# Second gate/up tile of the first feed-forward layer as seven block products

## The reference

```
x = x + L0_ffn(L0_cond(x))          # LoRA with 8 routed experts, then 4-bit weights
x = x + L1_ffn(L1_cond(x))          # one of 8 weight matrices per batch, then RMSNorm and FFN

def L0_ffn(x):                      # HIDDEN 512, INTER 1376
    w_gu = scale[g] * (nibble - (zero[g] + 1))
    gate, up = split(x @ w_gu)
    h = silu(gate) * up
    return h @ w_d                  # w_d: 4-bit too
```

## Time and profile before

| what | value |
|---|---|
| median of 3 runs | 446.32 us (446.04 to 447.08) |
| profiled execution | 446.06 us, span 444.3 us |
| TensorE busy | 439.1 us, 99% of the span |
| VectorE busy | 341.6 us, 77% |
| ScalarE busy | 219.4 us, 49% |
| GpSimd busy | 188.9 us, 43% |
| granted TensorE clock | 0.999 |

### The profile page before, as it was taken

How to read it: one execution, slowest core, us unless ns; L and a number is a source line. 1 busy time by engine, 2 the same in 40 slices (tenths; PEclk the granted TensorE clock), 3 DMA queues, 4 the chain that set the end, 5 groups by cost and what they waited for, 6 DMA issues and landing times.

```text
span 444.3 us, 5507 instructions
## 1 busy us (share of the span) xinstructions
PE 439.1 (99%) x1946; PEld 358.6 (81%) x1946; DVE 341.6 (77%) x439; ACT 219.4 (49%) x283; POOL 188.9 (43%) x167
## 2 busy tenths in 40 slices
PE   8999999999999999999999999999999999999997
PEld 4688888888888888888888778888888888888885
DVE  4689997788777978948778567868688678999922
ACT  5415755666542213347677656466466554474200
POOL 2077887855008201900005778886997300000000
PEclk9999999999999999999999999999999999999999
DMA  8765133100008694386279517947668146986623
GB/s 292 182 210 162 44 105 107 49 1 1 1 4 276 191 352 204 131 327 252 97 260 333 211 47 238 287 166 217 226 212 273 63 137 261 351 288 177 231 90 142
DMA packets 30344, 79.96 MB, mean 180 GB/s; under 512 B 2497, under 2 KB 15585, under 8 KB 28657
## 3 DMA queue, kind: packets, MB, share of 16 engines
q1 hardware_dynamic: 26464, 68.04, 45.0%
q0 software_dynamic: 3280, 10.83, 7.8%
q10 hardware_dynamic: 576, 0.80, 0.6%
HBM read 58.95 MB, written 20.72 MB: 179 GB/s over the span
## 4 chain that ended last, share of the span: by engine, by line
PE 98%; DMA 1%; ACT 0%; DVE 0%; issue 0%
PE ps L1890 10%; PE ps L1892 10%; PE ps L1891 10%; PE ps L1635 10%; PE ps L1639 10%; PE ps L1636 10%; PE ps L1994 5%; PE ps L1992 5%; PE ps L1752 5%; PE ps L1750 5%; PE ps L1751 5%; PE ps L1993 5%; PE ps L1873 2%; PE ps L1871 2%; PE ps L1872 2%; DMA res<-in_xT 1%
## 5 line engine op out<-in xcount | busy, mean ns | idle before, releaser
L1635 PE MATMUL ps<-h_hi,ring_hi 128*128 128x512 f32 x152 | 59.1, 389 | 0.0
L1636 PE MATMUL ps<-h_lo,ring_hi 128*128 128x512 f32 x152 | 59.1, 389 | 0.0
L1088 DVE TENSOR_TENSOR ring_lo<-raw,ring_hi 128x1792 fp32r<-128x1792 f32 (+1 forms) x23 | 47.6, 2073 | 14.7 <-ACT ring_hi L725 14.7
L1890 PE MATMUL ps<-zt_hi,ring_hi 128*128 128x512 f32 x140 | 54.5, 390 | 0.4 <-issue 0.4
L1892 PE MATMUL ps<-zt_hi,ring_lo 128*128 128x512 f32 x140 | 54.5, 389 | 0.0
L1891 PE MATMUL ps<-zt_lo,ring_hi 128*128 128x512 f32 x140 | 54.5, 389 | 0.0
L1639 PE MATMUL ps<-h_hi,ring_lo 128*128 128x512 f32 x152 | 47.8, 389 | 0.0
L725 ACT ACTIVATE ring_hi<-raw 128x1792 fp32r<-128x1792 f32 (+1 forms) x23 | 36.7, 1594 | 22.3 <-PE ps L1892 10.1
L1636 PEld LDWEIGHTS ps<-h_lo,ring_hi 128*128 128x128 f32 x152 | 28.5, 188 | 6.0
L1635 PEld LDWEIGHTS ps<-h_hi,ring_hi 128*128 128x128 f32 x152 | 28.5, 188 | 5.9
L1639 PEld LDWEIGHTS ps<-h_hi,ring_lo 128*128 128x128 f32 x152 | 28.5, 188 | 5.9
(11 more groups left out here) (252 smaller groups left out, 1115.3 us busy)
## 6 DMA issues: line engine op xcount, KB each, us to landing
ad_raw<-in_w1T SPq DMA_DIRECT2D x8, 1024.0 KB, 6.3
wd<-down_weights SPq DMA_DIRECT2D x7, 1024.0 KB, 5.5
down_weights<-dhi SPq DMA_DIRECT2D x7, 896.0 KB, 4.4
down_weights<-dlo SPq DMA_DIRECT2D x7, 896.0 KB, 4.3
raw<-in_gu SPq DMA_DIRECT2D x12, 512.0 KB, 3.7
wd<-down_weights SPq DMA_DIRECT2D x7, 768.0 KB, 5.1
draw<-in_d SPq DMA_DIRECT2D x7, 512.0 KB, 5.4
dn_work<-in_qw_dn SPq DMA_DIRECT2D x11, 256.0 KB, 4.7
```

Of the source, the lines that this page charges most:

```text
L1088: dve.tensor_tensor(dst, src, hi_part.bitcast(F32), ALU.subtract).then_inc(done_sem, 1)
L1635: pe.matmul(ps[:, bank + hf, :], w_hi, v_hi[:, t], start=first, stop=False)
L1636: pe.matmul(ps[:, bank + hf, :], w_hi, v_lo[:, t], start=False, stop=False)
L1890: pe.matmul(ps[:, bank, :], ring1_hi[s][:, w], z_hi[:, t], start=first and k == 0, stop=False, skip_group_check=True)
```

## The change

Tile 1 becomes a block tile (`BLOCK_TILES` from 1, `PLAIN` without it), with frame number 0 of the block tiles. What its frame needs is written in front of the loop: TensorE issues its six products without a product 4 of a predecessor, ScalarE and VectorE get its snapshots, additions, silus and product. On GpSimd `sums_gu(1)` is added and the gathers of pair 2 move behind it, those of pair 4 ahead of `sums_gu(3)`. On ScalarE `w_hi(1)` moves behind the splits of y, and `w_hi(2)` ahead of tile 1's snapshots. On VectorE `w_lo(1)` moves behind the splits of y, the dequantisation of tile 3 behind the low part of the third activation sum, and tile 0's low part of h into tile 2.

```diff
@@ -57,10 +57,10 @@
 YT = 11
 ZW = FT0 * 16
 
-BLOCK_TILES = tuple(range(2, FT0 - 2))
+BLOCK_TILES = tuple(range(1, FT0 - 2))
 NS = len(BLOCK_TILES)
 S_COL = {B_S1: 8 * P, B_S2: 10 * P, B_S3: 12 * P}
-PLAIN = (0, 1, FT0 - 2, FT0 - 1)
+PLAIN = (0, FT0 - 2, FT0 - 1)
 NPAIRS = FT0 // 2
 TD_GROUPS = (2, 2, 4, 3)
 
@@ -160,7 +160,7 @@
         scale = [region(kb, f"scale{j}", [P, KD, 4 * P], F32) for j, kb in enumerate((108, 48, 108, 48, 56))]
         scale.append(region(64, "scale_last", [P, KD, 2 * P], F32))
         nib = region(116, "nib", [P, FT0 * 2 * P], F32)
-        sil = {i: region(kb, f"sil{i}", [P, T], F32) for i, kb in zip(PLAIN, (100, 104, 180, 172))}
+        sil = {i: region(kb, f"sil{i}", [P, T], F32) for i, kb in zip(PLAIN, (100, 180, 172))}
         y_raw = region(184, "y_raw", [P, KD, T], F32)
         yt_hi = region(0, "yt_hi", [P, 4, 2, HALF], F32R)
         yt_lo, yt_raw = region(16, "yt_lo", [P, 4, 2, HALF], F32R), region(16, "yt_raw", [P, 4, 2, HALF], F32)
@@ -667,15 +667,16 @@
                 pool.wait_ge(s_wf, i + 1)
                 sums(sum_at("q", i), *blocks0(i % 2))
 
-            for j in range(3):
-                scales_gu(j)
+            scales_gu(0)
+            scales_gu(1)
+            sums_gu(1)
+            scales_gu(2)
             sums_gu(2)
+            scales_gu(4)
             sums_gu(3)
             scales_gu(3)
             pool.dma_start(lnb[:, :], a["lnw"].partition_broadcast(P)).then_inc(s_ln, 16)
             sums_gu(4)
-            scales_gu(4)
-            sums_gu(5)
             scales_gu(5)
             for i in BLOCK_TILES[4:]:
                 sums_gu(i)
@@ -824,24 +825,29 @@
                 act.activation(snap0[i % 2][:, 1, :], snap0[i % 2][:, 1, :], ACT.Silu).then_inc(s_silu1, 1)
 
             w_hi(0)
-            w_hi(1)
             y_split(0, 0)
             y_split(1, 4)
             y_copy(0, 0, 1)
             y_split(2, 6)
             y_split(3, 2)
+            w_hi(1)
             y_copy(3, 2, KD)
             y_copy(1, 4, KD)
             y_copy(2, 6, KD)
             y_sum_hi(1)
+            y_sum_hi(2)
             silu(0)
-            y_sum_hi(2)
+            y_sum_hi(3)
             w_hi(2)
-            y_sum_hi(3)
+            act.wait_ge(s_yt, 4)
+            y_snap_1(1)
+            y_snap_5(1)
             y_sum_hi(4)
+            y_snap_2(1)
+            y_silu_0(1)
             h_split(0)
-            silu(1)
-            for i in BLOCK_TILES:
+            y_silu_1(1)
+            for i in BLOCK_TILES[1:]:
                 y_snap_1(i)
                 w_hi(i + 1)
                 y_snap_5(i)
@@ -1295,13 +1301,12 @@
             dequant_gu(0)
             dequant_gu(1)
             w_lo(0)
-            w_lo(1)
             y_split(0, 0)
             y_split(1, 4)
             dequant_gu(2)
             y_split(2, 6)
             y_split(3, 2)
-            dequant_gu(3)
+            w_lo(1)
             b11, b12 = y_raw[:, 0:2, first], y_raw[:, 0:2, second]
             b21, b22 = y_raw[:, 2:4, first], y_raw[:, 2:4, second]
             dve.wait_ge(s_yr, 3)
@@ -1314,19 +1319,22 @@
             dve.tensor_tensor(y_low(yt_raw, 4), b21, y_low(yt_raw, 2), ALU.subtract).then_inc(s_yt, 1)
             y_sum_lo(1)
             y_sum_lo(2)
+            y_sum_lo(3)
+            dequant_gu(3)
+            y_c_11(1)
             gate_times_up(0)
             w_lo(2)
-            y_sum_lo(3)
+            y_c_12(1)
             y_sum_lo(4)
-            h_split(0)
-            for i in BLOCK_TILES:
+            y_c_22(1)
+            y_mul_1(1)
+            for i in BLOCK_TILES[1:]:
                 dequant_gu(i + 2)
-                if i > 2:
-                    y_mul_0(i - 1)
-                else:
-                    gate_times_up(i - 1)
+                y_mul_0(i - 1)
                 w_lo(i + 1)
                 y_c_11(i)
+                if i == 2:
+                    h_split(0)
                 h_split(i - 1)
                 y_c_12(i)
                 y_c_22(i)
@@ -1758,8 +1766,8 @@
 
             def y_p_1(i):
                 weights_ready(i)
-                if i < 4:
-                    pe.wait_ge(s_hm, i - 1)
+                if i == 2:
+                    pe.wait_ge(s_hm, plain(0) + 1)
                 need(pe, s_hm0, frame(i) - 1)
                 y_product(1, i % 2, 0, True, "b11").then_inc(s_p[1], 1)
 
@@ -1801,14 +1809,16 @@
             gate(0, range(KD), s_ylo)
             pe.wait_ge(s_yr, 2)
             up(0)
-            weights_ready(1)
             pe.wait_ge(s_yr, KD)
-            gate(1, range(KD))
-            up(1)
-            for i in BLOCK_TILES:
+            y_p_1(1)
+            y_p_2(1)
+            y_p_5(1)
+            y_p_6(1)
+            y_p_3(1)
+            y_p_7(1)
+            for i in BLOCK_TILES[1:]:
                 y_p_1(i)
-                if i > BLOCK_TILES[0]:
-                    y_p_4(i - 1)
+                y_p_4(i - 1)
                 y_p_5(i)
                 y_p_2(i)
                 y_p_6(i)
```

## The result

The changed kernel takes 451.04 us (median of 7 runs, 448.85 to 451.56), the kernel before beside it 446.12 us (7 runs, 445.66 to 447.08). The ratio is 1.0096, 95% interval 1.0084 to 1.0108: slower by about 1%, in the direction forecast and beyond the range. The seven times form two groups, three at 448.85 to 448.94, which lie inside the range, and four at 451.04 to 451.56, which don't. The profiled execution took 448.87 us, span 447.1, and belongs to the lower one.

What follows compares the result with a forecast made beforehand. The prediction took TensorE, 98% of the chain that ended last, to bound the kernel, with VectorE next. Its terms, +0.61 + 0.55 + 0.4 = +1.6 us, gave a forecast of 447.8 us, range 446.2 to 449.8.

Steps and rivals of the forecast that it cites:

- TensorE -1.36: TensorE in tile 1: 48 matmuls become 42 at 0.227 us each, -1.36 us.
- Front edge nothing: Ahead of tile 1's products: the added w_hi(1) and w_lo(1) fit into free slots and cost nothing.
- The cover on VectorE: VectorE ahead of the first activation sum: w_lo(1) ends near 49.45, 0.1 us before that sum at 49.55.
- VectorE's chain: VectorE from 56.02, without slack: w_lo(2) ends at 64.31, c22 at 66.65, so TensorE waits 0.99 and 0.98 us.
- The stall at product 6: TensorE at product 6 of tile 1, waiting for ScalarE's first snapshot: some 0.2 us, absorbed by the next term.
- Entry: TensorE through tiles 1 and 2: matmuls saved and two new waits, -1.36 + 0.99 + 0.98 = +0.61 us before any collision.
- Collision +0.55: GpSimd's sums(3) beside VectorE's w_lo(2), low part 4 and product of tile 1: one meeting, +0.55 us, bounds 0 to +2.1.
- Tile 2, lateness +0.4, bounds 0 and 1.5: From tile 2's product 4 on: sums(3) and sums(4) possibly late for the next weight splits, +0.4 us, bounds 0 and +1.5.
- the rival on GpSimd: Pair 4's gathers push sums(3) to sums(5) late, delaying TensorE's products 4 by up to 1 us; 449.5 to 450, chance 0.22.
- GpSimd as the late engine: Pair 4's gathers push sums(3) to sums(5) behind w_hi(3) to w_hi(5), delaying products 4; 449.5 to 450 us, chance 0.22.
- Waits in tiles 4 to 8 would show me wrong: Sign against the forecast: TensorE's waits repeat in tiles 4 to 8, where tiles from 4 on were expected at 9.52 us.

Runs made afterwards that it cites:

- the forced run: Changed kernel with one wait added: GpSimd's first sum of tile 2 starts only when VectorE's w_lo(1) is done; ratio 1.0147.
- the nearest, +1.3: Changed kernel with scales of pairs 3, 4, 5 loaded by one transfer each and VectorE's gate times up of tile 0 behind c22; ratio 1.0042.

## Why the prediction was wrong, point by point

- **TensorE -1.36.** Right: the forty-two matmuls of tile 1 stand at 0.227 us each but for the gaps.
- **Front edge nothing.** Right for TensorE: product 1 of tile 1 starts at 55.12, 10.88 us after tile 0, without a gap. The cover on VectorE did not hold: `w_lo(1)` met a sum, took 2.67 us, and the first activation sum began at 49.92 instead of 49.55. The four sums made that up, and the low parts behind them began at 56.08, forecast 56.02.
- **VectorE's chain.** Right to 0.1 us on the clock of the profile: `w_lo(2)` forecast to start at 62.29 and end at 64.31, measured 62.35 and 64.36; c22's end 66.65, measured 66.70; products 1 and 4 forecast at 64.4 and 66.75, measured 64.47 and 66.84. The stall at product 6 was 0.74 instead of 0.2, and was absorbed as said; what it took, product 1 of tile 2 did not wait. Entry +0.9, forecast +0.61 without a collision: TensorE's tile 0 began 0.13 us earlier than in before, so the same times mean longer waits, and the rest is product 4's 0.1 us and what the restarts cost.
- **Collision +0.55.** `w_lo(2)` took 2.01 in the profile, since the sums of tile 3 began at 61.66 with one sum of 0.76 and the next lost to VectorE (2.60); 2.45 in the runs where the sums came earlier. In the profiled run the term measured nothing; where it happened it was right in size, +0.45 against +0.55.
- **Tile 2, lateness +0.4, bounds 0 and 1.5.** This step failed: the term came to +2.3. The end of `sums(4)`, forecast at 77 to 80, was 78.82. The mistake was to stop there. `sums(5)` stand behind one more set of gathers (2.72 us for one of them), end at 90.62, and make `w_hi(5)` wait 3.69 us; I had them only in the rival on GpSimd. And I priced a late `w_hi` by when VectorE's `w_lo` and the c22 behind it are wanted, while the snapshot queued behind it on ScalarE comes due first. With the meeting at 47.3 us lost the term was +4.1, in the forced run; the prediction let the sums of tile 2 meet `w_lo(1)` without putting a price on the outcome. The median lies in the upper group, whose 2.3 us more are likely, though not shown, to be that meeting.
- **The rivals.** GpSimd as the late engine, at 0.22, is what happened, by product 3 and not by product 4, as I had it. Its price of 449.5 to 450 lies between the two groups. "Waits in tiles 4 to 8 would show me wrong" was the right test: tile 4 has two.
- **Where the expected gain is.** 1.36 us are saved. The entry, bound by VectorE, takes back 2.3, GpSimd's gathers most of another 2.3. Without the gathers' lateness the collision takes part of their place. No variant brought the stretch under the kernel before's; the nearest, +1.3, holds at least 0.3 us that come from how it loads its scales.

## What to carry to other kernels

When a step is moved up on an engine that was on time with 1 us to spare, follow that engine to the point where it waits for nothing again, and not only to the first deadline; and for each late result look at what is queued behind its reader. A saving on the bound engine is worth only the slack of its suppliers at that place: here 1.36 us of matmuls were taken out where VectorE was already busy 10.73 of 10.88 us. Where two engines meet within 0.03 us, expect that either can go first, and forecast both.

## What the runs showed of the hardware

- **The price of a meeting.** A GpSimd sum of 256 columns takes 0.73 us alone and 2.60 to 2.62 when a `w_lo` goes ahead of it; `w_lo`, 2.02 alone, takes 2.45 to 2.67 when a sum goes ahead, and took 3.07 beside two. A queue of sums can hold VectorE longer: the dequantisation at 86.63 took 3.40 us instead of 1.22 while four sums started at 86.81 to 89.08.

```profile
86.63 3.40 DVE L1231 SCALAR_TENSOR_TENSOR raw<-nib,scale 128x1024 f32<-128x1024 uint8 x1
```

- **Gathers slow down too, by who starts first.** An indirect gather takes 0.95 us on GpSimd with VectorE in PSUM work or idle. All the long ones (1.75 to 2.72 us in the changed kernel's profile) start while a VectorE instruction with two SBUF inputs runs; one that starts 0.02 us ahead of such an instruction keeps its 0.95. Here one of each, the second 0.13 us behind the start of `w_lo(4)`:

```profile
70.31 0.95 POOL L630 DMA_INDIRECT scale<-in_sc_gu,idx_gu  x1 [0.30 <-issue]
...
81.09 2.72 POOL L630 DMA_INDIRECT scale_last<-in_sc_last,idx_gu  x1 [0.30 <-issue]
```

```profile
70.33 2.03 DVE L1094 TENSOR_TENSOR ring_lo<-raw,ring_hi 128x1792 fp32r<-128x1792 f32 x1 [0.55 <-ACT ring_hi L726]
...
80.96 2.03 DVE L1094 TENSOR_TENSOR ring_lo<-raw,ring_hi 128x1792 fp32r<-128x1792 f32 x1 [0.45 <-ACT ring_hi L726]
```

- **A plain load can hold up a gather.** A gather with two plain loads of scales started 1.2 and 1.6 us behind it landed after 7.4 us in four profiles of four; the same gather took 4.0 to 4.4 us in five profiles without these loads beside it.
- **A wait can cost the clock.** In the forced run TensorE waited 4.30 us at the start, and its next matmuls of 512 columns stood 0.42 to 0.43 us apart instead of 0.227. The granted clock was 0.50 from 37.80 to 42.00, the lower of its two levels (1.2 and 2.4 GHz), and back at 1.00 from 44:

```profile
37.85 0.80 PE L1644 MATMUL ps<-act_hi,w0b_hi 128*128 128x512 f32 x1 [4.30 <-issue]
38.45 0.63 PE L1645 MATMUL ps<-act_lo,w0b_hi 128*128 128x512 f32 x1
38.87 0.63 PE L1644 MATMUL ps<-act_hi,w0b_hi 128*128 128x512 f32 x1
```

The waits in the block tiles, 1.23 us the longest of the changed kernel's profile, left it at 1.00.
